# Four-layer convolution kernel: first layer with 25 instead of 27 rounds of products a group, its inner input rows copied side by side

## The reference, cut to what matters

```python
def _denoise_block(x, w1, b1, w2, b2, w3, b3, a, b, c):
    trip = _triplets(x)                     # previous, own and next channel
    B, T, C, H, W = trip.shape              # 4, 16, 3, 512, 512
    xf = trip.reshape(B * T, C, H, W)
    o = a * _conv_reflect(xf, w1, b1, 1, 2) + b * _conv_reflect(xf, w2, b2, 2, 4) \
        + c * _conv_reflect(xf, w3, b3, 4, 8)
    return jnp.tanh(o).reshape(B, T, H, W)

x = x + _L0_conv_ref(_gn(x), ...)           # two denoise blocks, one after the other
```

## Time and profile before

| | |
|---|---|
| median of 3 runs | 5376.93 us (5367.36 to 5379.23) |
| profiled execution | span 5383.9 us, the time of that execution from its first to its last instruction |
| TensorE busy (PE) | 4994.9 us, 93% |
| its weight loads (PEld) | 3092.8 us, 57% |
| VectorE (DVE) | 3365.2 us, 63% |
| ScalarE (ACT) | 2396.6 us, 45% |
| GpSimd (POOL) | 1362.4 us, 25% |
| products of layer 0 (L679) | 55296 matmuls, 3027.2 us |
| DMA | 1166.78 MB, mean 217 GB/s |

### The profile page before, as it was taken

One profiled execution on the slowest core, in us unless ns is written; L12 is line 12 of the kernel. 1 busy time (PEld: TensorE's weight loads), 2 busy tenths in 40 slices (PEclk: granted clock), 3 DMA queues, 4 the chain that ended last, 5 costly groups with the idle time before them and its releaser, 6 DMA issues. The chain is left out here.

```text
span 5383.9 us, 178367 instructions
## 1 busy us (share of the span) xinstructions
PE 4994.9 (93%) x78653; PEld 3092.8 (57%) x78653; DVE 3365.2 (63%) x6195; ACT 2396.6 (45%) x2999; POOL 1362.4 (25%) x1629
## 2 busy tenths in 40 slices
PE   4998999899899999999999997998777799999998
PEld 2444444444447569997666663443556466666665
DVE  5543444344342555555555546887999788888888
ACT  1222222222221111111111117885999689899997
POOL 0000000000001111111111100000777355555556
PEclk9999999999999999999999998999999999999999
DMA  8677777777666767667667657998688366666664
GB/s 246 217 228 235 224 228 232 223 223 237 222 209 199 226 200 239 207 203 236 203 208 236 205 178 277 321 325 302 256 308 309 129 152 152 150 150 153 151 152 120
DMA packets 366864, 1166.78 MB, mean 217 GB/s; under 512 B 60457, under 2 KB 61096, under 8 KB 287018
## 3 DMA queue, kind: packets, MB, share of 16 engines
q1 hardware_dynamic: 363928, 1152.98, 69.0%
q10 hardware_dynamic: 2162, 2.39, 0.2%
HBM read 683.58 MB, written 453.51 MB: 211 GB/s over the span
## 5 line engine op out<-in xcount | busy, mean ns | idle before, releaser
L679 PE MATMUL c_p<-c_w,wc 128*32 128x512 f16 x55296 | 3027.2, 381 | 91.1 <-DMA c_w<-xs 81.1
L679 PEld LDWEIGHTS c_p<-c_w,wc 128*32 128x32 f16 x55296 | 1896.0, 97 | 1194.4 <-DMA c_w<-xs 76.2
L739 ACT ACTIVATE c_t<-c_p,cbias,cscale 128x512 f32<-128x512 f32 x512 | 397.9, 777 | 2582.6 <-PE c_p L679 2582.6
L591 DVE TENSOR_SCALAR c_y<-c_t 128x512 f16<-128x512 f32 x256 | 109.2, 426 | 855.1 <-ACT c_t L739 854.1
L601 DVE TENSOR_TENSOR a_x<-c_t,a_x 128x512 f32<-128x512 f32 x256 | 221.3, 865 | 666.7 <-ACT c_t L739 658.5
L1699 PE MATMUL f_P<-f_qh,f_wt 64*64 64x512 f16 x4608 | 545.7, 378 | 1.8 <-DVE f_t L1595 1.8
L1699 PE MATMUL f_P<-f_hl,f_wt 64*64 64x512 f16 x4608 | 545.3, 379 | 0.0
L1860 POOL TENSOR_TENSOR f_y<-f_y,f_x 128x512 f32<-128x512 f32 x256 | 330.7, 1292 | 449.3 <-DVE f_hl L1574 443.2
L1595 DVE SCALAR_TENSOR_TENSOR f_t<-f_P,f_kk,f_ci 128x256 f32<-128x256 f32 x1024 | 423.4, 476 | 12.8 <-PE f_P L1699 7.6
L810 POOL COPY c_y<-c_y 128x16 f16<-128x16 f16 x512 | 85.6, 197 | 1360.7 <-DVE c_y L593 1360.7
L1459 POOL TENSOR_TENSOR e_hl<-e_g,e_hl 128x2048 f16<-128x2048 f32 x63 | 257.1, 4081 | 609.3 <-ACT e_hl L1409 609.3
(11 more groups left out here) (263 smaller groups left out, 5887.4 us busy)
## 6 DMA issues: line engine op xcount, KB each, us to landing
c_w<-xs SPq DMA_DIRECT2D x576, 264.0 KB, 5.6
c_w<-ys SPq DMA_DIRECT2D x576, 264.0 KB, 4.0
d_x<-x SPq DMA_DIRECT2D x128, 1024.0 KB, 7.6
x<-d_x SPq DMA_DIRECT2D x128, 1024.0 KB, 5.1
ys<-c_y SPq DMA_DIRECT2D x576, 132.0 KB
xs<-a_hl SPq DMA_DIRECT2D x70, 1056.0 KB, 9.8
a_x<-in_x SPq DMA_DIRECT2D x256, 256.0 KB, 6.8
a_x<-in_x SPq DMA_DIRECT2D x128, 512.0 KB, 5.2
```

The costliest lines, as they stand in the source:

```text
L679: t = p.matmul(pg[32 * j:32 * j + 32, :], wu[:, blk, wl, var, di, :], buf[:, bk, xl * PW + PAD + dx:xl * PW + PAD + dx + NW], start=(di == ...
L739: s.activation(tt_[n % 3][:, :], pp[:, n % 4, :], ACT.Tanh, bias=cbias[:, blk:blk + 1], scale=cscale[:, blk:blk + 1]).then_inc(c_act, 1)
```

## The change

The rows of a window are put in another order: in `slot` the 16 own rows stand in partitions 0 to 63, the four rows above and the four below in 64 to 95, the outer ones in 96 to 127. The inner 24 rows thus fill 96 partitions, and for the horizontal shifts of 1 and 2 no others have a weight.

For each group three copies by VectorE and one by ScalarE make two tiles: `near` has the high halves of the 96 partitions and, in the last 32, the low halves of partitions 64 to 95; `twice` has the low halves of the 16 own rows in partitions 0 to 63 and the same ones, displaced by 3 columns, in 64 to 127. For the four shifts of 1 and 2 the 12 rounds become 10: four with the low weights on the window, four with `near`, and two with `twice`, each of which serves two shifts. `products` is now 5 * 3 + 4 + 4 + 2 = 25 rounds; 19 read the window, then come waits on the copies. The weights `wn` for `near` and `twice` are copied from `wc` by GpSimd at the start. The copies for group n + 1 stand on both engines ahead of the work on group n, and wait until the products of group n - 1 are done and, with the first group of a unit, until the window of that unit has landed. A load of one group and one pair of channels is four transfers, of 32, 16, 8 and 8 rows, of the same bytes in all.

```diff
@@ constants: slot
-        h8, s = ((1, 0), (0, 0), (1, 1), (0, 1))[row // 8 + 1]
-        v8 = row + 8 * h8 - 16 * s
-        return 8 * (2 * v8 + chan % 2) + 4 * s + 2 * h8 + chan // 2
+        place = row if 0 <= row < 16 else 16 + (row + 4 if -4 <= row < 0 else row - 12 if row >= 16 else row + 20)
+        return 4 * place + 2 * (chan % 2) + chan // 2
@@ layer0
+        near = [sb(ctx, f"c_n{i}", [128, 4, PW], F16) for i in range(2)]
+        twice = [sb(ctx, f"c_2{i}", [128, 4, PW], F16) for i in range(2)]
+        def rows_in(e, n):
+            u, g = divmod(n, 4)
+            if u == 0:
+                e.wait_ge(c_l0[g // 2], 256)
+            elif g == 0:
+                e.wait_ge(c_ld[u % 2], n_win(u))
+            if n >= 2:
+                e.wait_ge(c_pe, n - 1)
+            return win[u % 2][:, 4 * g:4 * g + 4]
@@ vector
+                def copies(n):
+                    w = rows_in(v, n)
+                    v.tensor_copy(near[n % 2][0:96], w[0:96, :, 0:PW]).then_inc(c_nh, 1)
+                    v.tensor_copy(near[n % 2][96:128], w[64:96, :, PW:RW]).then_inc(c_nl, 1)
+                    v.tensor_copy(twice[n % 2][0:64], w[0:64, :, PW:RW]).then_inc(c_2a, 1)
...
                     for g in range(4):
                         i, s = stage_of(u, g)
+                        if 4 * u + g + 1 < 8 * NU:
+                            copies(4 * u + g + 1)
@@ tensor: products
-                    for di, dx in enumerate(DX):
-                        for z, (wl, xl) in enumerate(((0, 0), (0, 1), (1, 0))):
...
+                    for di in (4, 0, 1, 7, 8):
+                        for wl, xl in ((0, 0), (0, 1), (1, 0)):
+                            four(wu[:, blk, wl, :, di], rows4, xl * PW + PAD + DX[di], start=(di, wl, xl) == (4, 0, 0))
+                    for di in (2, 3, 5, 6):
+                        four(wu[:, blk, 1, :, di], rows4, PAD + DX[di])
+                    if n == 0:
+                        p.wait_ge(w_wn, 12)
+                    p.wait_ge(c_nh, n + 1)
+                    p.wait_ge(c_nl, n + 1)
+                    for e, di in enumerate((2, 3, 5, 6)):
+                        four(wn[pr % 2][:, blk, :, e], near[n % 2], PAD + DX[di])
+                    p.wait_ge(c_2a, n + 1)
+                    p.wait_ge(c_2b, n + 1)
+                    four(wn[pr % 2][:, blk, :, 4], twice[n % 2], PAD - 2)
+                    t = four(wn[pr % 2][:, blk, :, 5], twice[n % 2], PAD - 1, stop=True)
@@ scalar
+                def copies(n):
+                    w = rows_in(s, n)
+                    s.activation(twice[n % 2][64:128, :, PAD - 2:PAD - 1 + NW], w[0:64, :, PW + PAD + 1:PW + PAD + 2 + NW], ACT.Copy).then_inc(c_2b, 1)
@@ sync: load
-                        for h8 in range(2):
-                            e.dma_start(win[half][gp % 2 + 2 * h8:128:4, 4 * g:4 * g + 4].rearrange("p k w -> p (k w)"),
-                                        dram(src, pair(b, gp, 0, 16 * half + 4 * g) + h8 * (8 * VP - RW),
-                                             [[CP, 16], [RW, 2], [1, 4 * RW]])).then_inc(c_ld[half] if u else c_l0[g // 2], 16)
+                        at = pair(b, gp, 0, 16 * half + 4 * g)
+                        for first, off, n in ((0, 0, 32), (80, RW, 16), (64, 12 * VP - RW, 8), (112, 8 * VP - RW, 8)):
+                            e.dma_start(win[half][first + gp % 2:first + 2 * n:2, 4 * g:4 * g + 4].rearrange("p k w -> p (k w)"),
+                                        dram(src, at + off, [[CP, n], [1, 4 * RW]])).then_inc(c_ld[half] if u else c_l0[g // 2], 16)
```

More of the change, by code:

```diff
@@ L379, in n_win @@
         def n_win(u):
-            return 128 * sum(1 + (place(r)[2] == 0) for r in range(u % 2, u + 1, 2) if r)
+            return 256 * sum(1 + (place(r)[2] == 0) for r in range(u % 2, u + 1, 2) if r)
+        def rows_in(e, n):
[7 more added lines that the diff above has]
+            return win[u % 2][:, 4 * g:4 * g + 4]
         def table_of(u):
@@ L631, in _ @@
                 v0(2), v1(2)
+                copies(0)
                 for u in range(2 * NU):
@@ L673, in products, with four @@
                         p.wait_ge(c_act, n - 3)
-                    for di, dx in enumerate(DX):
-                        for z, (wl, xl) in enumerate(((0, 0), (0, 1), (1, 0))):
-                            for j in range(4):
-                                bk = 4 * g + j
-                                var = 0 if (half, bk) == (0, 0) else (2 if (half, bk) == (1, 15) else 1)
-                                t = p.matmul(
-                                    pg[32 * j:32 * j + 32, :], wu[:, blk, wl, var, di, :],
-                                    buf[:, bk, xl * PW + PAD + dx:xl * PW + PAD + dx + NW],
-                                    start=(di == 0 and z == 0), stop=(di == 8 and z == 2), tile_position=(0, 32 * j))
+                    def four(weights, source, at, start=False, stop=False):
+                        for j in range(4):
+                            bk = 4 * g + j
+                            var = 0 if (half, bk) == (0, 0) else (2 if (half, bk) == (1, 15) else 1)
+                            t = p.matmul(pg[32 * j:32 * j + 32, :], weights[:, var], source[:, j, at:at + NW],
+                                         start=start, stop=stop, tile_position=(0, 32 * j))
+                        return t
+                    rows4 = buf[:, 4 * g:4 * g + 4]
+                    for di in (4, 0, 1, 7, 8):
[13 more added lines that the diff above has]
+                    t = four(wn[pr % 2][:, blk, :, 5], twice[n % 2], PAD - 1, stop=True)
                     t.then_inc(c_pe, 1)
```

23 lines of the change are left out of this document (18 added, 5 removed).

## The result

The changed kernel takes 5458.4 us (median of 4 runs, 5447.1 to 5465.5). The kernel before, on the same chip, took 5378.1. The ratio is 1.014, 95% interval 1.011 to 1.017: slower by 80 us, where I forecast 27 us less. The profiled execution has a span of 5463.7 us, against 5383.9.

A forecast was written before the change was run, and what follows sets the result against it. TensorE alone was taken to bound block 2, TensorE and four DMA engines level block 1. 5383.9 - 101 (block 2) + 75 (block 1) = 5358 us, given as 5351 for the median; own range 5310 to 5390, 8 in 10 5275 to 5425.

The forecast's parts named there:

- Block 2: Second block of layer 0, bound by TensorE: two rounds fewer a group save 110.6 us, less 10 us of charges, -101 us.
- Rival C: VectorE's copies run at half the speed: +260 us in block 2, some 80 in block 1, about 5700 us; chance 0.04.
- The wait of `p0` in block 1: TensorE's idle time before `p0(i)` grows from 1.40 to 3.7 us, since copies stand ahead of v0; low clock costs 1.7 us.
- The loads: Block 1's window loads, four transfers for two: the 8-row ones run on 8 engines, the quarter among them; +82 us.
- 5 us at the start: Block 1: eight more load issues of 0.64 us stand ahead of the first product, +5 us.
- Rival A: The 8-row loads are spread over all engines, so block 1's DMA work stays as it is; 5285 us, chance 0.22.
- a share near 0.5: Sign in block 1: windows with a DMA share near 0.5 from 8-row loads, beside those of 0.26.
- TensorE's own path for eight groups is 49.5 us: Block 1, one tile prepared beside eight groups: 48.99 - 3.46 + 2.3 + 1.7 us; the two rounds' gain is given back.
- Rival B: Block 1: copies queued behind `hi(i)` and v0 come late, TensorE stops for `near` or `twice`; 5432 us, chance 0.22.
- TensorE's stalls over this are idle time for windows, so the clock and `p0` cost nothing further: Block 1 at about +75 us: TensorE's waits beyond its own path are for windows, so clock and `p0` add nothing.
- Slower: Outcome slower than the kernel before by more than 0.2% (11 us); chance 0.26.

The follow-up runs named there:

- b_8rows: The kernel before, with one of its two 32-row window loads cut into 16, 8 and 8 rows; 5447.3 us, ratio 1.013.
- b_4x16: The kernel before, with both 32-row window loads cut into two of 16 rows; 5408.8 us, ratio 1.006.
- a_lay: The changed kernel with `ys` written by image row, so the 64 rows of a store lie at one distance; 5361.6 us, ratio 0.996 against the kernel before.
- b_lay: The kernel before with `ys` written by image row and four loads of 16 rows for two in block 2; 5313.1 us, ratio 0.987.
- a_late: The changed kernel with block 1's copies for the next group put behind `evict` and `halves`; 5522.6 us, ratio 1.026 against the kernel before.
- a_lay_vq: a_lay_v with the stores to `ys` issued by GpSimd; 5278.4 us, ratio 0.982 against the kernel before.
- a_lay_v: a_lay with v0 and v1 ahead of the copies on VectorE; 5291.8 us, ratio 0.983 against the kernel before.
- b_ysq: The kernel before with the stores to `ys` issued by GpSimd, behind the pads, instead of SyncE; 5370.2 us, ratio 0.998.
- v01_first: The changed kernel with v0 and v1 ahead of the copies on VectorE; 5449.8 us, ratio 1.013 against the kernel before.

## Why the prediction was wrong

*Block 2: right.* -93 us for -101. The copies take 0.70 to 0.72 us (0.70 forecast), the first of three 0.81 on average, and up to 1.60; VectorE is busy for 0.96 (0.9 or more). Nothing waits on the copies there. Rival C, copies at half the speed, is out.

*The wait of `p0` in block 1: right in size.* The idle time is 3.9 us for 3.7 in 25 of 29 cases, with a clock below 1 behind it. In the set shown that clock costs 1.7 us, as forecast; over the 25 it costs 1.7 to 2.9.

*The loads: the sum near, its cause half.* The +82 us were meant for block 1 and for nothing but 8-row loads on half of the engines. b_8rows, where nothing else changes, is slower by 67, of which 52 are in block 1; and 8 rows instead of 16 cost 39. The other 28 come with smaller transfers and twice the issues, for which I had no term beyond 5 us at the start. So what I priced is half as large, and that the sum is near is in part luck. Rival A, in which 8-row loads cost nothing, is out. But the sign I had named for 8 engines, a share near 0.5, tells nothing: 41 of the 560 windows of the changed kernel lie between 0.46 and 0.54, and so do 31 of the kernel before, which has no such load, and 54 of b_4x16. On how many engines an 8-row load runs isn't shown.

*"TensorE's own path for eight groups is 49.5 us": short by 1.6.* a_lay has the copies without the four-engine stores, and 23 of its 28 sets take 49.6 to 51.5 us, 15 of them 51.0 to 51.2; the clock behind `p0` costs more there than my 1.7. But the set shown of the changed kernel takes 54.9. What is missing from the path is no work of TensorE's: I followed v0 past the copies and not v1, which stands behind the next unit's copies, and they wait for a window. In the changed kernel `p1_` stops 23 times for it, in a_lay, where windows come earlier, 5 times (39.5 us). Rival B had the queue the other way round, with the copies behind `hi(i)` and v0, which wait for transfers, and looked for the stop at `near` and `twice`; there it is 25 us in all. It is at `p1_`, and 121 us.

*"TensorE's stalls over this are idle time for windows, so the clock and `p0` cost nothing further": this step failed.* I took the time of block 1 as the longer of two paths, so that what one loses is hidden under the other. It wasn't hidden: `p0` cost 72 us more, the clock some 97, the new stops at `p1_` 121, and the idle time for windows, which should have taken them in, fell by 28. Runs with one part each show the same. Block 1 is 1579 us in b_lay. With the four-engine stores it is 1659 (the kernel before, +80). With the change and spread stores it is 1712 (a_lay, +133). With both it is 1834, +255, more than the 213 of the two together. b_8rows, with loads cut as in the changed kernel and no copies, is 1711. So the longer of the two paths would be 1712, by either reckoning, and 1834 came. My reading is that the two take turns: the copies wait for a window (ScalarE 466 us, VectorE 314), what is queued behind them comes late, TensorE stops, a group ends late, and the next loads, which wait for it, start late. That the losses aren't hidden is shown; this chain is shown only as far as v1 and `p1_`, the rest is argued. Of the +175 us of block 1 in the table, 52 are there with the loads alone, and 40 go with the copies' time. The other 83 have no single owner, and the three are differences between unlike kernels, not parts that must add up. v0 and v1 behind the copies are 17 us of block 1 with four-engine stores, and 67 with the others. Whether a late eviction behind ScalarE's copy is the rest stays open, since a_late couldn't tell.

*The chances.* Slower had 0.26, most of it with B, whose number was near: its 5432 are the forecast and 81 us, so +156 in block 1, for +166 measured. Its mechanism, waits for transfers passed on through the queues of VectorE and ScalarE, is nearest to what came, but it had them in the wrong order and at the wrong tiles, so that the number is as near is in part luck.

A version that beats both kernels came out of it: a_lay_vq with 5278 us (0.982, 0.980 to 0.984), and a_lay_v with 5292, which can't be told from it for certain. Most of the gain is the layout's: b_lay alone has 5313. With it the change and the new order are worth 21 us more (a_lay_v against b_lay).

## What to carry to other kernels

Where two resources are level, don't take the longer of their two times: ask whether their waits fall at the same moment, and if not, add them (here the two together cost even more than the sum). When an instruction that waits for a transfer is put into an engine's queue, go through all that stands behind it until the next such wait, each with its consumer, not only the first; here its wait cost more than its duration. Look at the outermost dimension of every transfer's two patterns, and at the DMA share where few transfers are open: here a share that stood at 0.24 to 0.27 and never went to zero was work that a quarter of the engines did alone.

## What the runs showed of the hardware

- A load of 16 rows described as 2 by 8 ran on two engines: share 0.12 to 0.13, 52 to 55 GB/s, and layer 0 took some 1970 us more than in the changed kernel. This pattern cost more than all else in this study.
- The same stores issued by GpSimd fall into more packets. From 300 to 900 us b_ysq has 28418 packets under 512 bytes where the kernel before has 5909, and a DMA share of 0.82 for 0.72, at 229 and 228 GB/s. It was faster in spite of that, by 10 us.
- What a short stop costs at TensorE's clock varied. At full clock 76 matmuls take 4.28 us. In a_lay `p0` has 26 stops of 3.9 us, and behind them 76 matmuls took 5.55 to 7.18 us. In v01_first it has 24 stops of 1.8 us, and behind them they took 4.29 us in 11 cases and 5.97 in 13. Behind the four stops of `p1_` up to 1.6 us in the changed kernel they took 4.29. So a stop of 3.9 us cost 1.3 to 2.9 us more through the clock, a third to three quarters of the stop itself.
